# A fused decoder layer: the turns of the MLP's inner rows one cell later, the down projection at the slot's end, its residual in the next slot

## The chip, the cores and the metric

One core of one Trainium2 chip runs the whole kernel. The metric is the device time of one execution in microseconds (us). The engines are PE (TensorE, matmuls; its weight loads are PEld), DVE (VectorE), ACT (ScalarE), POOL (GpSimd) and SP (SyncE, which here only issues transfers). Each runs its own list of instructions in order, and they wait for one another by semaphores. PE writes into eight PSUM banks.

## The reference: what is computed

One decoder layer on x of 8 batches x 512 rows x 512 columns, in float32:

```
x = x + self_attention(layernorm(x))             16 heads of 32, causal, q and k normed per head
x = x + cross_attention(layernorm(x), ctx_1024)  16 heads, softmax over the 32 largest scores
x = x + ffn(layernorm(x))

ffn: gate = silu(bitlinear(x, w_gate)); up = bitlinear(x, w_up)     inner width 2048
     return bitlinear(gate * up, w_down)
bitlinear(x, w): rows of x rounded to 8-bit steps of their largest element, w to -1, 0, 1
```

The inner rows h = gate * up are 2048 wide. The down projection needs each row's largest element over all 2048 before it can round any of them.

## The kernel before

The program is a pipeline written out by hand. Time is cut into **slots** s = -7 to 160. Slot s handles one group of four heads of one tile of 128 query rows in self attention, and of cross attention 20 slots later (`LAG`). A batch is 16 slots. Each slot has eight **cells**, 0 to 7: the even ones carry a head of self attention, the odd ones a head of cross attention. In each cell PE turns the probabilities (`probs`, L595), computes scores (`scores`, L627 to L632), multiplies the head of the cell before by its values (`values`, L609), and then does the **units** that `cells(s)` puts into the cell: projections of q, k and v, turns (transposes) of inputs and of attention results, the output projections, and the MLP's matmuls. Units use two PSUM banks in turn (`shared_ps`), so a unit waits (`freed`) until the unit two before it has been read: mostly by ACT, for the output projections and the down projection by DVE.

The MLP of a row tile t takes three slots (`mlp_step`, r = 0, 1, 2), from slot 37 of a batch's own count on:

- r = 0 and 1: gate and up projections for four chunks of 512 (cells 2 and 6). ACT reads them (L742), POOL completes the silu (`silu`, L1115 and L1117), DVE multiplies by up and finds the maximum (`mlp`, L968 and L971). The last chunk, at cell 6 of r = 1, is finished by POOL and DVE in the following slot, with each row's scale (L977 to L982).
- r = 2, here called the **down slot**: POOL quantises the inner rows in four pieces (`inner_quant`, L1129), PE turns each piece (unit `hT`, L637 with `hh`) in cells 2, 3, 4 and 5, ACT copies them to `hT` (L742), and PE runs the down projection of 16 matmuls in cell 6 (unit `down`, L672). DVE's last step in the slot (`down`, L989) scales it and adds the residual `x2res`. SP stores the result at the start of the next slot (`store_y`, L503).

The down slots are s mod 16 = 7, 10, 13 and 0 for t = 0, 1, 2 and 3. The last batch's MLP runs nearly alone, in slots 149 to 160: the **tail**.

What else stands in these slots matters. On DVE each slot is in the main the search for the 32 largest scores of four heads (`top`, L878 and L883: 32 passes over 128x512). In between come `self_maxima` (L1019), `norms` (L900 and L909, which divide attention results by their sums; they need the values of both kinds of heads up to the last cell of the slot before), `mlp`, `row_scale`, `cross_rows` (L926) and `self_rows` (L939, which adds the input to the output projection of self attention, L656). The self output projection is in cell 3 of slots 14, 15, 0 and 1 mod 16, the turn of its input in cell 2. In slot 0 cell 3 also holds a projection `self_qkv` (L684, 8 matmul records), in slot 10 the cross queries (L703), in slot 7 cells 2 and 3 hold the turns of self keys and queries (L707), and in slot 13 cell 5 holds the cross values (L696). The order of DVE's steps in a slot is this list:

```
top(c, 0, FIRST_MAX)
self_maxima(s - 1, 1)
top(c, 0, ROUND_1)
sum_squares(s)
norms(s)
mlp(s - 1, False)
top(c, 0, ROUND_2)
...
```

SP's list in a slot: inputs, the stores of x1 and x2, `store_y` of the slot before, the residual loads `x1res` and `xres`, the residual load `x2res` of a down slot, the weights, and the copies of turned keys and queries to their stacks (`copy_part`, L513, 32 transfers in a slot that has them).

Of the kernel before, what the change touches and what calls it, by code (L numbers as in the profile page):

```python
# [16 lines left out]
NB, S, D = 8, 512, 512  # L17
# [9 lines left out]
SLOTS = NG * NT  # L27
# [4 lines left out]
RING = 3  # L32
REPLACED = -3e38
LAG = 20
FIRST, LAST = -7, SLOTS * (NB - 1) + LAG + 28
CELLS = 2 * HG
NS = NB * SLOTS
NTILES = NB * NT
# [30 lines left out]
def cross_tile(s):  # L69
    return tile_at(s, LAG + 15)  # L70
# [44 lines left out]
def mlp_down(s):  # L115
    t, r = mlp_step(s)
    return [t] if t is not None and r == 2 else []


def cells(s):  # L120

    u = [[] for _ in range(CELLS)]
    g, q = self_group(s), s % NT
    if g is not None:
        for at, cell, unit in ((0, 0, ("self_qkv", g, 0)), (0, 3, ("self_qkv", g, 1)), (0, 6, ("self_qkv", g, 2)),
                               (1, 1, ("self_qkv", g, 3)), (3, 2, ("self_kT", g)), (3, 3, ("self_qT", g))):
            if at == q:
                u[cell].append(unit)
    g = cross_group(s)
    if g is not None:  # L130
        for at, cell, unit in ((1, 5, ("cross_v", g)), (2, 0, ("cross_kT", g)), (2, 3, ("cross_qT", g))):
            if at == q:
                u[cell].append(unit)
    if cross_tile(s) is not None:
        u[0].append(("cross_oT", cross_tile(s)))
        u[1].append(("cross_out", cross_tile(s)))
    if x1_tile(s) is not None:
        u[1].append(("feed", "x1", x1_tile(s)))
    if self_tile(s) is not None:
        u[2].append(("self_oT", self_tile(s)))  # L140
        u[3].append(("self_out", self_tile(s)))
    if x2_tile(s) is not None:
        u[4].append(("x2T", x2_tile(s)))
    for early, cell in ((True, 2), (False, 6)):
        for t, n in mlp_chunk(s, early):
            u[cell] += [("gate", t, n), ("up", t, n)]
    for t in mlp_down(s):
        for n in range(NF):
            u[2 + n].append(("hT", t, n))
        u[6].append(("down", t))  # L150
    for k, f in enumerate(feeds(s)):
        u[5 + k].append(("feed", *f))
    return u
# [108 lines left out]
def decoder_layer(nc, x, ctx_in, W_attn, b_attn, W_proj, b_proj, q_gamma, q_beta, k_gamma, k_beta,  # L262
# [10 lines left out]
    with ExitStack() as keep:  # L273
# [77 lines left out]
        hT = sb("hT", [P, KF, P], BF16)  # L351
# [14 lines left out]
        def pipeline():  # L366
            C = Counts()
# [51 lines left out]
            for s in slots:  # L419
                t = self_tile(s)  # L420
                if t is not None:
                    for k in ("x1", "stats", "aggr"):
                        C.plan("x1_stats", (k, t))
                    for k in range(5):
                        C.plan("x1_norm", (t, k))
                t = x2_tile(s)
                if t is not None:
                    for k in ("amax", "clip", "inv"):
                        C.plan("dve_rows", (k, t))
                    for k in range(3):  # L430
                        C.plan("pool_rows", ("quant", t, k))
                t = cross_tile(s)
                if t is not None:
                    for k in ("x2", "stats", "aggr"):
                        C.plan("dve_rows", (k, t))
                    for k in range(6):
                        C.plan("pool_rows", ("ln", t, k))
                for early, at in ((False, s - 1), (True, s)):
                    for t, n in mlp_chunk(at, early):
                        C.plan("h_pool", ("t1", t, n))  # L440
                        C.plan("h_pool", ("r", t, n))
                        C.plan("h_dve", ("h", t, n))
                        C.plan("h_dve", ("max", t, n))
                        if n == NF - 1:
                            for k in ("amax", "clip", "inv"):
                                C.plan("h_dve", (k, t))
                            C.plan("h_pool", ("scale", t))
                            for q in range(NF):
                                C.plan("h_pool", ("q", t, q))
                for t in mlp_down(s):  # L450
                    C.plan("h_dve", ("out", t))

            def freed(eng, u):

# [25 lines left out]
            with nc.Block() as block:  # L480
                @block.sync
                def _(sp):
# [18 lines left out]
                    def store_y(t):  # L501
                        sp.wait_ge(h_dve, upto("h_dve", ("out", t)))
                        sp.dma_start(rows(out_rows, t), x2res[:]).then_inc(y_out, step("y_out", t, 16))  # L503
# [15 lines left out]
                    for s in slots:  # L519
                        done += len(feeds(s - 1))  # L520
                        while pending and ring[pending[0]] - RING < done:
                            load_feed(pending.pop(0))
                        t = x1_tile(s)
                        if t is not None:
                            sp.wait_ge(x1_stats, upto("x1_stats", ("x1", t)))
                            sp.dma_start(rows(x1_rows, t), xres[:]).then_inc(x1_out, step("x1_out", t, 16))
                        t = x2_tile(s)
                        if t is not None:
                            sp.wait_ge(dve_rows, upto("dve_rows", ("x2", t)))
                            sp.dma_start(rows(x2_rows, t), x2t[:]).then_inc(x2_out, step("x2_out", t, 16))  # L530
                        for t in mlp_down(s - 1):
                            store_y(t)
                        t = cross_tile(s)
                        if t is not None:
                            if t:
                                sp.wait_ge(dve_rows, upto("dve_rows", ("x2", t - 1)))
                            sp.wait_ge(x1_out, upto("x1_out", t, 16))
                            sp.dma_start(x1res[:], rows(x1_rows, t)).then_inc(x1res_in, step("x1res_in", t, 16))
                        t = self_tile(s)
                        if t is not None:  # L540
                            if t:
                                sp.wait_ge(x1_out, upto("x1_out", t - 1, 16))
                                sp.wait_ge(x1_norm, upto("x1_norm", (t - 1, 4)))
                            sp.dma_start(xres[:], rows(x_rows, t)).then_inc(xres_in, step("xres_in", t, 16))
                        for t in mlp_down(s):
                            sp.wait_ge(x2_out, upto("x2_out", t, 16))
                            if t:
                                sp.wait_ge(y_out, upto("y_out", t - 1, 16))
                            sp.dma_start(x2res[:], rows(x2_rows, t)).then_inc(x2res_in, step("x2res_in", t, 16))
                        for at, which, g, before in loads:  # L550
                            if at == s:
                                load_weights(which, g, before)
                        mine = [u for cell in cells(s) for u in cell if u[0] in STACKED]
                        if mine:
                            k_unit, q_unit = mine
                            for unit, j in ((k_unit, 0), (k_unit, 1), (q_unit, 0), (q_unit, 1),
                                            (k_unit, 2), (q_unit, 2), (k_unit, 3), (q_unit, 3)):
                                copy_part(unit, j)
                    for t in mlp_down(LAST):
                        store_y(t)  # L560
                    sp.wait_ge(x1_out, 16 * NTILES)
                    sp.wait_ge(x2_out, 16 * NTILES)
                    sp.wait_ge(y_out, 16 * NTILES)
# [301 lines left out]
                def _(dve):  # L865
# [156 lines left out]
                    for s in slots:  # L1022
                        c = s - LAG
# [3 lines that stand above are left out]
                        sum_squares(s)  # L1027
                        norms(s)
                        mlp(s - 1, False)
                        top(c, 0, ROUND_2)  # L1030
                        row_scale(s)
                        cross_rows(s)
                        top(c, 0, ROUND_3)
                        top(c, 1, FIRST_MAX)
                        self_maxima(s, 0)
                        self_rows(s)
                        top(c, 1, ROUND_1)
                        feed_stats_of(s + 1)
                        top(c, 1, ROUND_2)
                        mlp(s, True)  # L1040
                        top(c, 1, ROUND_3)
                        down(s)

                @block.gpsimd
                def _(pool):
# [424 lines left out]
```

## Time and profile before

| | |
|---|---|
| median of 3 runs | 4032.62 us (4030.38 to 4032.8) |
| the profiled execution | 4034.79 us, its span 4033.0 us |
| busy: PE, DVE, ACT, POOL | 3329.4, 3343.9, 2450.5, 1796.7 us |
| mean granted TensorE clock | 0.859 of full speed |
| chain that ended last, by engine | DVE 40%, PE 25%, POOL 13%, issue 11% |

The span is cut by the profile into instructions on each engine with start, duration, and what ended the idle time before them. "A <- B" means that A's engine stood idle until B was done. Idle time of an engine costs only where the end of the program hangs on that engine, so each wait has to be looked at in its place. The granted clock is the share of TensorE's full clock of 2.4 GHz that it was given.

### The profile page before, as it was taken

The numbers are of one execution on the slowest core, as the hardware profiler recorded it, in microseconds if no ns is written. First come the engines' busy times: TensorE is split into PE (matmuls) and PEld (weight loads), VectorE is DVE, ScalarE is ACT, GpSimd is POOL, SyncE is SP. The second block draws the span as 40 slices with busy tenths as digits, with TensorE's granted clock in tenths as the row PEclk, the third lists the DMA queues.
The fourth block names the chain that finished last, engine by engine and source line by source line (L and its number), as shares of the span: only waits on it lengthen the run. The fifth ranks groups of instructions, "written<-read, shape, count | busy, mean of one in ns | idle before, by whom it ended". The sixth has DMA issues, their size and how long they took to land.

```text
span 4033.0 us, 61337 instructions
## 1 busy us (share of the span) xinstructions
PE 3329.4 (83%) x18502; PEld 2434.3 (60%) x18502; DVE 3343.9 (83%) x7699; ACT 2450.5 (61%) x4921; POOL 1796.7 (45%) x2316
## 2 busy tenths in 40 slices
PE   2587898998989898998899888997899888877775
PEld 2365576666666666666666666666666666555542
DVE  4312299999999899899989999999989999999962
ACT  3344476666766567666766676666766676455533
POOL 0123244445654555444544555445544554344433
PEclk7768888888988899888988898898988898877767
DMA  7122322322222212222223222222232221211100
GB/s 271 52 54 64 99 64 76 84 77 60 77 77 72 70 49 79 79 73 69 74 77 84 63 71 67 74 65 62 77 89 79 58 66 43 61 45 35 32 21 19
DMA packets 167443, 283.04 MB, mean 70 GB/s; under 512 B 40639, under 2 KB 52939, under 8 KB 166606
## 3 DMA queue, kind: packets, MB, share of 16 engines
q1 hardware_dynamic: 160782, 275.98, 25.1%
q10 hardware_dynamic: 6336, 3.15, 0.3%
q8 instruction: 153, 2.51, 0.3%
q14 instruction: 172, 1.41, 0.1%
HBM read 113.27 MB, written 31.46 MB: 36 GB/s over the span
## 4 chain that ended last, share of the span: by engine, by line
DVE 40%; PE 25%; POOL 13%; issue 11%; ACT 4%; SPq 3%; DMA 1%; DVEq 0%; POOLq 0%; ACTq 0%
DVE cW L883 17%; DVE top L878 13%; PE bank L684 5%; PE bank L656 4%; PE bank L609 4%; POOL srs L1149 4%; SPq L513 3%; PE bank L672 2%; DVE smx L1019 2%; PE bank L637 2%; POOL cS L1170 2%; PE bank L595 2%; DVE hh L968 2%; POOL hh L1117 1%; DVE hmx L971 1%
## 5 line engine op out<-in xcount | busy, mean ns | idle before, releaser
L883 DVE MATCH_REPLACE8 cW<-top,cW 128x512 f32<-128x512 f32 x1536 | 1026.8, 676 | 0.0
L878 DVE MAX8 top<-cW 128x8 f32<-128x512 f32 x1536 | 981.4, 681 | 0.0
L799 ACT ACTIVATE PT<-bank 128x512 f32<-128x512 f32 (+3 forms) x1024 | 537.9, 525 | 356.5 <-PE bank L595 353.1
L1170 POOL TENSOR_TENSOR cS<-cS,cW 128x512 f32<-128x512 f32 x512 | 667.7, 1325 | 185.4 <-ACT cW L827 185.3
L609 PE MATMUL bank<-cv,PT 128*128 128x33 f32 x4096 | 585.0, 290 | 138.7 <-ACT PT L799 138.1
L609 PEld LDWEIGHTS bank<-cv,PT 128*128 128x128 f32 x4096 | 552.8, 209 | 176.5 <-ACT PT L799 170.2
L1177 POOL TENSOR_SCALAR cnb<-top 128x2 f32<-128x2 f32 x256 | 49.0, 191 | 938.1 <-DVE top L878 924.3
L609 PEld LDWEIGHTS bank<-sv,PT 128*128 128x128 f32 x2560 | 397.4, 211 | 82.2 <-ACT PT L799 59.6
L827 ACT ACTIVATE cW<-cW,cnb 128x512 f32<-128x512 f32 x512 | 348.7, 737 | 110.5 <-DVE cW L883 110.3
L684 PE MATMUL bank<-w_group,xT 128*128 128x384 f32 x1024 | 411.6, 550 | 0.0
L609 PE MATMUL bank<-sv,PT 128*128 128x33 f32 x2560 | 373.3, 280 | 36.7 <-ACT PT L799 35.6
L595 PE MATMUL bank<-ident,cS 128*128 128x128 f32 x2048 | 350.1, 298 | 63.2 <-POOL cS L1170 63.2
L821 ACT ACTIVATE cS<-cS,cnb 128x512 f32<-128x512 f32 x512 | 379.6, 741 | 16.1 <-DVE cW L883 16.1
L1019 DVE TENSOR_REDUCE smx<-sP 128x2 f32<-128x256 f32 (+3 forms) x256 | 205.9, 804 | 212.7 <-ACT sP L808 212.7
L1163 POOL TENSOR_TENSOR part<-part 128x512 fp32r<-128x512 f32 x128 | 168.3, 1315 | 451.1 <-ACT part L742 450.9
L595 PEld LDWEIGHTS bank<-ident,cS 128*128 128x128 f32 x2048 | 279.9, 162 | 116.7 <-POOL cS L1170 67.3
L883 DVE MATCH_REPLACE8 cW<-top,cS 128x512 f32<-128x512 f32 x512 | 342.5, 677 | 0.0
L878 DVE MAX8 top<-cS 128x8 f32<-128x512 f32 x512 | 327.2, 681 | 5.7 <-ACT cS L808 5.7
L814 ACT ACTIVATE sP<-sP,snb 128x384 f32<-128x384 f32 (+3 forms) x512 | 294.9, 578 | 35.5 <-POOL snb L1184 34.8
L808 ACT ACTIVATE cS<-bank 128x512 f32<-128x512 f32 x512 | 311.8, 609 | 1.6 <-PE bank L632 1.6
L684 PEld LDWEIGHTS bank<-w_group,xT 128*128 128x128 f32 x1024 | 205.2, 211 | 137.2 <-issue 40.3
L632 PE MATMUL bank<-ck_stack,cq_stack 128*128 128x512 f32 x512 | 269.1, 526 | 5.8 <-ACT cS L808 4.4
(151 smaller groups left out, 6092.4 us busy)
## 6 DMA issues: line engine op xcount, KB each, us to landing
sk_stack<-part SPq DMA_DIRECT2D x512, 64.0 KB, 2.0
sq_stack<-part SPq DMA_DIRECT2D x512, 64.0 KB, 2.0
ck_stack<-part SPq DMA_DIRECT2D x512, 64.0 KB, 2.0
cq_stack<-part SPq DMA_DIRECT2D x512, 64.0 KB, 2.0
w_group<-wa_by_group SPq DMA_DIRECT2D x32, 768.0 KB, 4.5
w_group<-wc_by_group SPq DMA_DIRECT2D x32, 768.0 KB, 4.3
feed<-in_x SPq DMA_DIRECT2D x32, 256.0 KB, 2.9
feed<-in_ctx SPq DMA_DIRECT2D x32, 256.0 KB, 3.0
```

The costliest lines, as they stand in the source:

```text
L595: mm = pe.transpose(turned_ps[C.parity("turned_full", label)][:, k * P:(k + 1) * P], p[:, k * P:(k + 1) * P], ident[:])
L609: mm = pe.matmul(o[:, j * (HD + 1):(j + 1) * (HD + 1)], pt[:, k * P:(k + 1) * P], v[m // NT % len(v)][:, k, j, :], start=k == 0, stop=k == ...
L684: mm = pe.matmul(ps[:, 0:3 * P], xT[:, c, t * P:(t + 1) * P], w_group[:, c, :], start=False, stop=c == NC - 1, skip_group_check=True)
L799: act.activation(PT[k][:, 0:n], turned_ps[k][:, 0:n], ACT.Copy).then_inc(turned_read, step("turned_read", label))
L808: act.activation(dst, score_ps[k][:, 0:n], ACT.Copy).then_inc(score_read, step("score_read", label))
L814: act.activation(p, p, ACT.Exp, bias=snb[:, j:j + 1], scale=SCALE).then_inc(sexp, step("sexp", (m, j)))
L821: act.activation(cS[c % 2][j][:], cS[c % 2][j][:], ACT.Exp, bias=cnb[c % 2][:, j:j + 1], scale=SCALE).then_inc(cexp, step("cexp", (c, j)))
L827: act.activation(cW[j][:], cW[j][:], ACT.Exp, bias=cnb[c % 2][:, j:j + 1], scale=SCALE).then_inc(crest, step("crest", (c, j)))
L878: dve.max(top8[:, j, r, :], src[:]).then_inc(topk, step("topk", (c, r, "max", j)))
L883: dve.match_replace(cW[j][:], top8[:, j, r, :], src[:], REPLACED).then_inc(topk, step("topk", (c, r, "replace", j)))
L1019: dve.reduce_max(smx[:, 2 * half:2 * half + 2], sP[half][:, :, 0:n], AXX).then_inc(smax, step("smax", (s, half)))
L1170: pool.tensor_tensor(cS[m % 2][j][:], cS[m % 2][j][:], cW[j][:], ALU.subtract).then_inc(cprob, step("cprob", (m, j)))
```

## The change

The units `hT` of a down slot move from cells 2 to 5 to cells 3 to 6, and the unit `down` from cell 6 to cell 7, the last. DVE's out step for it moves from the end of the down slot to the next slot, behind `norms` and `mlp(s - 1, False)`. SP's store moves with it, to the end of that next slot. The pipeline gets one slot more (to 161) for the last out step.

```
-FIRST, LAST = -7, SLOTS * (NB - 1) + LAG + 28
+FIRST, LAST = -7, SLOTS * (NB - 1) + LAG + 29
...
     for t in mlp_down(s):
         for n in range(NF):
-            u[2 + n].append(("hT", t, n))
-        u[6].append(("down", t))
+            u[3 + n].append(("hT", t, n))
+        u[7].append(("down", t))
...
+                for t in mlp_down(s - 1):
+                    C.plan("h_dve", ("out", t))
                 for early, at in ((False, s - 1), (True, s)):
...
-                for t in mlp_down(s):
-                    C.plan("h_dve", ("out", t))
...
                             sp.dma_start(rows(x2_rows, t), x2t[:]).then_inc(x2_out, step("x2_out", t, 16))
-                        for t in mlp_down(s - 1):
-                            store_y(t)
                         t = cross_tile(s)
...
                                 copy_part(unit, j)
-                    for t in mlp_down(LAST):
-                        store_y(t)
+                        for t in mlp_down(s - 1):
+                            store_y(t)
...
                         mlp(s - 1, False)
+                        down(s - 1)
                         top(c, 0, ROUND_2)
...
                         top(c, 1, ROUND_3)
-                        down(s)
```

The instructions are the same ones in another order; line numbers fall by two. On **PE, slot 80** (third batch, t = 3), from the turn of the self output (`so`) in cell 2 on; `hh` is a turn of inner rows, `cS` and `sP` are probabilities. Before:

```order
L637 MATMUL bank<-ident,so 128x128 x4
L637 MATMUL bank<-ident,hh 128x128 x4
L595 MATMUL bank<-ident,cS_1 128x128 x4
L632 MATMUL bank<-ck_stack,cq_stack 128x512
L609 MATMUL bank<-sv,PT 128x33 x4
L681 MATMUL bank<-bias,ones 128x128 x3
L684 MATMUL bank<-w_group,xT 128x384 x4
L653 MATMUL bank<-bias,ones 128x512
L656 MATMUL bank<-wproj,oT 128x512 x4
L637 MATMUL bank<-ident,hh 128x128 x4
```

After:

```order
L635 MATMUL bank<-ident,so 128x128 x4
L593 MATMUL bank<-ident,cS_1 128x128 x4
L630 MATMUL bank<-ck_stack,cq_stack 128x512
L607 MATMUL bank<-sv,PT 128x33 x4
L679 MATMUL bank<-bias,ones 128x128 x3
L682 MATMUL bank<-w_group,xT 128x384 x4
L651 MATMUL bank<-bias,ones 128x512
L654 MATMUL bank<-wproj,oT 128x512 x4
L635 MATMUL bank<-ident,hh 128x128 x4
```

The first turn of `hh`, which stood in front of cell 3, now stands behind its projection (L684, now L682) and the self output projection (L656, now L654).

On **PE at the end of slot 80**, before:

```order
L681 MATMUL bank<-bias,ones 128x128 x3
L684 MATMUL bank<-w_group,xT 128x384 x4
L672 MATMUL bank<-wdT,hT 128x512 x16
L637 MATMUL bank<-ident,feed 128x128 x4
L595 MATMUL bank<-ident,cS_3 128x128 x4
L632 MATMUL bank<-ck_stack,cq_stack 128x512
L609 MATMUL bank<-sv,PT 128x33 x4
```

After:

```order
L682 MATMUL bank<-w_group,xT 128x384 x4
L635 MATMUL bank<-ident,hh 128x128 x4
L635 MATMUL bank<-ident,feed 128x128 x4
L593 MATMUL bank<-ident,cS_3 128x128 x4
L630 MATMUL bank<-ck_stack,cq_stack 128x512
L607 MATMUL bank<-sv,PT 128x33 x4
L670 MATMUL bank<-wdT,hT 128x512 x16
```

The 16 matmuls on `wdT` leave cell 6; the last turn of `hh` takes their place, and they stand behind the last cell's scores and values, in front of the next slot's probabilities.

On **DVE, from the end of slot 80 into slot 81**, before:

```order
L883 MATCH_REPLACE cW<-top,cW 128x512 x2
L989 SCALAR_TENSOR_TENSOR x2res<-bank,hcol,x2res 128x512
L878 MAX top<-cS_0 128x8
L878 MAX top<-cS_1 128x8
L1019 TENSOR_REDUCE smx<-sP 128x2
L883 MATCH_REPLACE cW<-top,cS_0 128x512
L883 MATCH_REPLACE cW<-top,cS_1 128x512
L878 MAX top<-cW 128x8 x2
L900 RECIPROCAL rr<-bank 128x8
L909 TENSOR_TENSOR so<-bank,rr 128x128
L909 TENSOR_TENSOR co<-bank,rr 128x128
L883 MATCH_REPLACE cW<-top,cW 128x512 x2
```

After:

```order
L881 MATCH_REPLACE cW<-top,cW 128x512 x2
L876 MAX top<-cS_0 128x8
L876 MAX top<-cS_1 128x8
L1017 TENSOR_REDUCE smx<-sP 128x2
L881 MATCH_REPLACE cW<-top,cS_0 128x512
L881 MATCH_REPLACE cW<-top,cS_1 128x512
L876 MAX top<-cW 128x8 x2
L898 RECIPROCAL rr<-bank 128x8
L907 TENSOR_TENSOR so<-bank,rr 128x128
L907 TENSOR_TENSOR co<-bank,rr 128x128
L987 SCALAR_TENSOR_TENSOR x2res<-bank,hcol,x2res 128x512
L881 MATCH_REPLACE cW<-top,cW 128x512 x2
```

The out step (`x2res`) stands behind norms (L909, now L907), nine rows later.

On SP, in slot 78 for example, the store of `out_y` (L503) stands behind the load of `xres` (L544, now L542) and the 32 copies of keys and queries (L513), where it stood in front of them.

## Rows read from the trace of the kernel before

**Rows 1.** The page, part 1: busy us, share of the span, instructions.
```profile
PE 3329.4 (83%) x18502; PEld 2434.3 (60%) x18502; DVE 3343.9 (83%) x7699; ACT 2450.5 (61%) x4921; POOL 1796.7 (45%) x2316
```

**Rows 2.** Waits, whole span: engine line waited for, us in total, times, longest.
```profile
PE bank L637 <- POOL hh L1129: 165.1, 32, 9.3
...
DVE xres L939 <- PE bank L656: 103.2, 29, 7.0
...
DVE x2res L989 <- PE bank L672: 78.9, 27, 11.0
```

**Rows 3.** Line 989, window 840 to 3830: durations min/median/max, first, last; then its waits.
```profile
L989 DVE SCALAR_TENSOR_TENSOR x2res<-bank,hcol,x2res x28: 745/751/752, 985.1 to 3825.3; 128x512 f32<-128x512 f32 x28
...
  PE bank L672: 35.3, 23
```

**Rows 4.** Timeline of PE, slot 80: start, us, line, tiles, [idle before <-releaser].
```profile
2097.53 0.63 PE L637 MATMUL bank<-ident,hh 128*128 128x128 f32 x4 [2.24 <-POOL hh L1129]
...
2100.25 5.49 PE L684 MATMUL bank<-w_group,xT 128*128 128x384 f32 x8
...
2106.16 3.70 PE L656 MATMUL bank<-wproj,oT 128*128 128x512 f32 x8
...
2116.23 2.85 PE L684 MATMUL bank<-w_group,xT 128*128 128x384 f32 x8
```

**Rows 5.** Timeline of DVE, slots 48, 112, 128 and the end of 80.
```profile
1222.45 0.69 DVE L939 TENSOR_TENSOR xres<-bank,xres 128x512 f32<-128x512 f32 x1 [5.61 <-PE bank L656]
...
2122.57 0.75 DVE L989 SCALAR_TENSOR_TENSOR x2res<-bank,hcol,x2res 128x512 f32<-128x512 f32 x1 [2.21 <-PE bank L672]
...
2127.27 0.19 DVE L900 RECIPROCAL rr<-bank 128x8 f32<-128x8 f32 x1
...
2997.28 0.69 DVE L939 TENSOR_TENSOR xres<-bank,xres 128x512 f32<-128x512 f32 x1 [5.60 <-PE bank L656]
...
3432.05 0.69 DVE L939 TENSOR_TENSOR xres<-bank,xres 128x512 f32<-128x512 f32 x1 [3.73 <-PE bank L656]
```

**Rows 6.** Windows in slot 80: length, busy by engine, PEclk, DMA share, GB/s.
```profile
2095.30:2099.20 3.90, 1.67 (x15) 1.66 (x15) 3.80 (x12) 2.15 (x6) 3.65 (x6) 1.00 0.11 16
2099.20:2106.10 6.90, 6.90 (x16) 3.41 (x15) 5.09 (x12) 1.50 (x5) 0.58 (x3) 0.51 0.19 73
```

**Rows 7.** Timeline of PE, slot 87.
```profile
2300.14 1.09 PE L637 MATMUL bank<-ident,hh 128*128 128x128 f32 x4 [8.66 <-POOL hh L1129]
```

**Rows 8.** Timeline, PE and DVE, slots 90 and 91.
```profile
2376.63 1.09 PE L637 MATMUL bank<-ident,hh 128*128 128x128 f32 x4 [3.62 <-POOL hh L1129]
...
2394.09 0.75 DVE L989 SCALAR_TENSOR_TENSOR x2res<-bank,hcol,x2res 128x512 f32<-128x512 f32 x1 [1.33 <-PE bank L672]
...
2398.17 0.09 DVE L883 MATCH_VALUE_LOAD cW<-top,cS 128x8 f32 x1 [0.48 <-POOL cS L1170]
...
2400.47 0.28 DVE L909 TENSOR_TENSOR co<-bank,rr 128x128 f32<-128x128 f32 x1
...
2401.23 0.64 PE L707 MATMUL bank<-ident,sx 128*128 128x128 f32 x4
```

**Rows 9.** Timeline, PE and DVE, slots 77 and 78.
```profile
2010.25 1.09 PE L637 MATMUL bank<-ident,hh 128*128 128x128 f32 x4 [5.14 <-POOL hh L1129]
2012.70 1.09 PE L637 MATMUL bank<-ident,hh 128*128 128x128 f32 x4
...
2026.44 0.75 DVE L989 SCALAR_TENSOR_TENSOR x2res<-bank,hcol,x2res 128x512 f32<-128x512 f32 x1 [0.32 <-PE bank L672]
...
2032.95 0.28 DVE L909 TENSOR_TENSOR co<-bank,rr 128x128 f32<-128x128 f32 x1
...
2034.88 0.63 PE L637 MATMUL bank<-ident,so 128*128 128x128 f32 x4
...
2046.56 0.69 DVE L939 TENSOR_TENSOR xres<-bank,xres 128x512 f32<-128x512 f32 x1 [4.95 <-PE bank L656]
```

**Rows 10.** Line 989, window 3930 to 4033: its waits.
```profile
  PE bank L672: 43.6, 4
```

## The prediction

> **What bounds the kernel now.** I read the page first: PE and DVE are both busy 83% of the span [rows 1], so neither alone explains the time, and an edit that only moves work pays only where one of the two waits for the other. The list of waits is next [rows 2]. Three of its rows belong to the piece of program that moves: PE waits 165.1 us for POOL's quantised inner rows before it turns them, DVE waits 103.2 us for the output projection of self attention, and 78.9 us for the down projection. Which of these lies on the path is seen slot by slot in the timeline. The slots repeat by the batch: the same wait comes at 1222.45 and, four batches on, at 2997.28 [rows 5], a period of 443.7 us for 16 slots. A batch has four down slots, s mod 16 = 7, 10, 13 and 0, for the row tiles t = 0 to 3. 28 of the 32 down steps lie in the full slots, and there DVE waits 35.3 us for them [rows 3]; the other four are the last batch's, in the tail: 43.6 us [rows 10].
>
> In each of these down slots PE comes to the first turn at cell 2 while POOL has not quantised yet, and stands: 2.24 us in slot 80 [rows 4], 8.66 in 87 [rows 7], 3.62 in 90 [rows 8], 5.14 in 77 [rows 9]. Everything of PE behind it is late: in slot 80 the self output projection ends at 2106.16 + 3.70 = 2109.86, and DVE stands 5.6 us for it (five such slots, 5.61 to 5.58, and a sixth with 3.73), then 2.21 us for the down projection [rows 5]. These are DVE's only gaps in that slot, so in slot 80 DVE follows PE.
>
> **The change, part by part.** No instruction is added or removed; what is priced is order.
>
> *The turns move one cell back.* At cell 2 PE goes on to cell 3 instead of standing. What it gains is the work of cell 3 that now fits in front of POOL's answer, at most the stall. In slot 80 cell 3 holds two projections, 5.49 and 3.70 us [rows 4], more than the stall, so all 2.24 us go. In slot 90 it holds the projection of the cross queries, 8 matmuls of 512, so the 3.62 us go too. In slot 77 it is small: between the first and the second turn lie 2012.70 - 2010.25 = 2.45 us, 1.09 of them the turn itself [rows 9], so 1.4 us are gained and 3.7 us of stall stay. In slot 87 some 3 of the 8.66 us go; DVE does not follow PE there.
>
> *The clock in slot 80.* From 2095.3 to 2099.2, the stretch with the stall, PE is busy 1.67 of 3.90 us; in the 6.9 us after it the granted clock is 0.51, the lower level of 1.2 GHz [rows 6], and a projection of 8 matmuls takes 5.49 us where the same one takes 2.85 later [rows 4]. With the stall gone PE is busy through that stretch. Bounds for what this gives: 0 (the clock falls all the same) and 5.49 - 2.85 = 2.64 us. I take 2.64, because no other stall stands in front of the fall in this slot.
>
> *Slots 0 and 1, where DVE follows PE, gain what PE gains*: 2.24 + 2.64 = 4.9 us. DVE could take 5.61 + 2.21 = 7.8; the rest comes back as a wait at the reciprocal of norms in the next slot (at 2127.27 in [rows 5]), which needs attention values that PE computes after the down projection. Five such slots give 24.4 us. The sixth waited 3.73 us, the bound; I take 3. Together **27.4 us**.
>
> *The residual moves to the next slot.* Where DVE waits at its end only for the down projection, and PE has caught up by the next slot's norms, the wait goes in full; the 0.75 us instruction only changes slot. Of the 35.3 us, five waits of 2.21 (11.1) are those of slots 0, counted above, and six of 0.3 to 0.5, like the 0.32 in [rows 9] (2.5 in all), are slots 13. The other 35.3 - 11.1 - 2.5 = **21.7 us** are slots 7 and 10 (1.33 in [rows 8]). DVE has next to no gap in slots 8 to 13, so it keeps them.
>
> *Slots 13 and 14.* DVE follows PE again, to the 4.95 us wait in slot 78 [rows 9]: the gain is PE's 1.4 us, the 0.32 included. But the 3.7 us of stall that stay can draw a fall of the clock onto the value projection of cell 5. Bounds: 1.4 - 2.64 = -1.2 us (a loss as in slot 80) and 4.95 (the whole wait goes). I take half of 1.4, 0.7 us, nearest to the turn's own rows, six times: **4.2 us**. By the Trainium skill's page TensorE: Matmul & The Clock Gate, Part 1, the throttled state is the default and activity releases it; by that rule the remaining stall costs clock, each of these slots is at its lower bound, and the sum is 11 us smaller.
>
> *POOL.* In slot 90 PE turns and projects the next inputs earlier, POOL's chain behind them comes earlier, and DVE's 0.48 us wait for POOL's subtraction in slot 91 goes [rows 8], six times: **2.9 us**.
>
> *What could come onto the path: the bank.* The down projection's PSUM bank is now free only after DVE's out step, which comes behind norms, and PE's second unit after the down projection needs it. In slot 78 norms end at 2032.95 + 0.28 = 2033.2; DVE is 0.32 + 0.75 us earlier there, and with the 0.75 of the out step it is done at about 2033.0. PE reaches the unit, the turn of the self output, at 2034.88 [rows 9], or 1.4 us earlier: 0.5 us of cover. In slot 91 norms end at 2400.75, less 1.33 + 0.75, plus 0.75: 2399.4, and PE's turn of the keys is at 2401.23 [rows 8]: 1.8 us, against a lead that grows by up to 3.6. So PE is never later there than today, only its new lead can be cut: cost 0. The Trainium skill's page PSUM — Partial Sum Buffer, section Summary: rules for kernel authors, says "Evacuate promptly"; that speaks against holding a bank for some 6 us, and is the last rival below.
>
> *SP and the ends.* On SP the store of the result moves behind the residual load of self attention and behind the 32 part copies of slots 11 and 14. The next user of its buffer is a load two slots later, and the loads it stood in front of are freed: 0. In the tail the MLP's steps follow each other as before, so the four waits [rows 10] stay: 0. The added slot 161 holds only the last out step and store, which ended the program before too: 0.
>
> **Sum.** 27.4 + 21.7 + 4.2 + 2.9 = 56.2 us. The profiled execution took 4034.8 us, which gives 3978.6; it lies 2.2 us over the median of the runs, so the median comes to **3976 us**.
>
> **Rivals.**
> - *The clock falls all the same* (0.2). For: no row shows that this stall, and not the slot's load, lowered it. Then 5 x 2.24 + 2 = 13.2 instead of 27.4, and 0 instead of 4.2: 3976 + 18.4 = 3995 us.
> - *More than PE's own gain* (0.12): PE, earlier from slot 77 on, takes the rest of the 4.95 us wait in slots 14 as well, 6 x 4.25 = 25 us more: 3951 us. For: that wait is as long as the stall in slot 77 [rows 9]. Against: nothing in PE's work gets shorter.
> - *The waits return elsewhere* (0.1): DVE, early at norms in slots 8 and 11, stands there for the values behind the down projection. Then only what PE gains is left, 13.2 + 4.2 = 17.4: 4015 us. Against: PE is 3 us ahead there.
> - *It does nothing* (0.05): each wait that goes reappears before the slot ends: 4032 us.
> - *Slower* (0.06), by the held bank: PE stands at its second unit until DVE's out step. It decides once PE is the bound behind that point and its lead (3.6 us) exceeds the cover (0.5 to 1.8, about 1.2): 2.4 us in each of 28 down slots are 67 us against 56 gained, 4043 us. Against: only in slots 0 and 13 does DVE follow PE, and PE's lead is smaller there.
>
> **Numbers.** The forecast has the remaining 0.47. To hold 8 in 10, the range reaches over the first rival with slots 13 at their lower bound, and to the second: **3948 to 4010**. About 0.2% (8 us) can be told from no change in this kernel. Faster by over that: 0.47 + 0.2 + 0.12 + 0.1 = 0.89; within it 0.05; slower 0.06.
>
> **What would show it.** Right: PE's wait for POOL before the inner turns falls from 165 us to about 100, with none left in slots 0 and 10; the wait for the self output projection in slots 0 goes from 5.6 us to under 1, with the clock at 1.0; DVE's wait for the down projection is gone outside the tail; a wait of 1 to 3 us at the reciprocal appears in slots 1; the period falls from 443.7 to about 437 us. Wrong: a PE wait of over 1 us for DVE's out step in the slots after down slots, or the projection in slot 0 still at 5.5 us.

## The result, and the profile after

The changed kernel takes 3981.3 us (median of 4 runs, 3970.9 to 3984.7); the kernel before takes 4031.5 us (median of 4). The ratio is 0.9872, 95% interval 0.9852 to 0.9892: 50 us or 1.3% faster. The forecast was 3976 us, range 3948 to 4010. The profiled execution of the changed kernel is its fastest run, 3970.9 us (span 3968.7), 64 us below that of the kernel before, so slot times read from the two traces add up to more than the 50 us of the medians.

The waits of the whole span, with the columns of [rows 2]:

```profile
PE bank L635 <- POOL hh L1127: 97.4, 19, 9.3
...
DVE xres L937 <- PE bank L654: 81.1, 21, 8.0
...
DVE x2res L987 <- PE bank L670: 43.2, 4, 11.7
```

Line numbers are two lower than before. PE's wait for the quantised rows falls from 165.1 to 97.4 us, and 13 of its 32 occasions are gone. DVE's wait for the down projection is down from 78.9 to the 43.2 us of the tail. The wait for the self output projection falls by only 22.1 us in all, but in slots 0 it is gone: there it was 31.7 us in six slots before, five of about 5.6 and one of 3.73. In slots 14 it grew by 10.4 us, in slots 1 by 3.3. Where the out step stands now, line 987 over 840 to 3830 us ([rows 3] before):

```profile
L987 DVE SCALAR_TENSOR_TENSOR x2res<-bank,hcol,x2res x28: 741/741/750, 988.4 to 3765.7; 128x512 f32<-128x512 f32 x28
its engine sat idle before it (us, times) until:
who waited for it (us, times):
  PEld bank L705: 4.6, 5
  PE bank L705: 3.9, 5
...
  PE bank L662: 2.7, 2
...
  PE bank L635: 1.3, 1
```

Nothing is waited for in front of it any more, and PE now waits for it: 3.9 us in five slots 11, and 4.0 us in three slots near the end (123, 129 and 139). The prediction had named a PE wait of over 1 us there as a sign of being wrong; three of the eight are (1.03, 1.88 and 1.25 us).

Slot 80 as PE's timeline shows it, from the turn of the self output on ([rows 4]):

```profile
2072.15 0.63 PE L635 MATMUL bank<-ident,so 128*128 128x128 f32 x4
...
2074.47 2.85 PE L682 MATMUL bank<-w_group,xT 128*128 128x384 f32 x8
...
2077.57 3.70 PE L654 MATMUL bank<-wproj,oT 128*128 128x512 f32 x8
...
2081.10 0.60 PE L635 MATMUL bank<-ident,hh 128*128 128x128 f32 x4
```

There is no stall, and the first projection takes 2.85 us, not 5.49. The windows of slots 77 and 80 say what the clock was (columns as in [rows 6]; the granted clock is the third number from the end). Before:

```profile
2002.17:2027.10 24.93, 19.79 (x129) 16.17 (x128) 24.44 (x60) 12.78 (x30) 12.78 (x16) 0.86 0.10 33
...
2088.65:2123.24 34.59, 32.35 (x174) 22.23 (x173) 26.53 (x63) 16.77 (x38) 12.82 (x20) 0.90 0.20 58
```

After:

```profile
1978.59:2002.46 23.87, 19.26 (x117) 16.79 (x116) 23.70 (x60) 13.64 (x32) 12.78 (x16) 0.79 0.14 45
2066.14:2092.07 25.93, 25.72 (x158) 19.31 (x158) 25.69 (x62) 16.69 (x38) 12.83 (x20) 1.00 0.28 77
```

Slot 80 runs at the full 2.4 GHz; slot 77 runs longer at 1.2 GHz than before. The lower clock now reaches the value projection behind the first turn of inner rows. Before, the first of its four pieces took as long as the others:

```profile
2016.44 1.16 PE L696 MATMUL bank<-w_group,ctxT 128*128 128x128 f32 x8
```

After, the first turn, the first two pieces, and DVE's wait in slot 78, which was 4.95 us before ([rows 9]):

```profile
1986.68 1.08 PE L635 MATMUL bank<-ident,hh 128*128 128x128 f32 x4 [4.30 <-POOL hh L1127]
...
1992.58 1.99 PE L694 MATMUL bank<-w_group,ctxT 128*128 128x128 f32 x8
...
1994.65 1.16 PE L694 MATMUL bank<-w_group,ctxT 128*128 128x128 f32 x8
```

```profile
2024.42 0.69 DVE L937 TENSOR_TENSOR xres<-bank,xres 128x512 f32<-128x512 f32 x1 [6.79 <-PE bank L654]
```

In the table a slot is the time from its first `top` pass on DVE to the next slot's, in the batch of slots 68 to 83. Slots 0 and 1 are 80 and 81 there, in the profile of each kernel.

| slots mod 16 | before | after | difference | forecast |
|---|---|---|---|---|
| 0 and 1 | 34.6 + 23.6 | 25.9 + 27.0 | -5.2 | -4.9 |
| 7 and 8 | 35.9 + 24.3 (34.7 + 24.3 in most batches) | 30.7 + 24.1 | -5.3 (-4.2 in most) | -1.9 |
| 10 and 11 | 26.5 + 25.7 (27.7 + 25.7 in some) | 25.6 + 25.7 | -0.8 or -2.1 | -0.5 to -1.8 |
| 13 and 14 | 24.9 + 31.2 | 23.9 + 33.7 | +1.5 | -0.7 |
| period, mean of four | 443.7 | 433.6 | -10.1 | about -9 |

### The profile page after: what moved, and what is told of

It is laid out like the page before. It is cut to its first block, busy times and chain, and to the rows that moved or that the text cites. A ratio compares the mean times of both kernels' runs of the same rounds, so it can differ in the third digit from the quotient of the medians.

```text
span 3968.7 us, 61337 instructions
## 1 busy us (share of the span) xinstructions
PE 3343.2 (84%) x18502; PEld 2462.5 (62%) x18502; DVE 3333.4 (84%) x7699; ACT 2460.3 (62%) x4921; POOL 1789.4 (45%) x2316
## 4 chain that ended last, share of the span: by engine, by line
DVE 42%; PE 26%; issue 10%; POOL 10%; ACT 4%; SPq 3%; DMA 1%; DVEq 0%; POOLq 0%; ACTq 0%
DVE cW L881 18%; DVE top L876 14%; PE bank L682 6%; PE bank L607 5%; PE bank L654 4%; SPq L513 3%; POOL srs L1147 3%; PE bank L593 2%; DVE smx L1017 2%; PE bank L670 2%; DVE hh L966 2%; PE bank L635 2%; POOL cS L1168 1%; DVE hmx L969 1%; POOL hh L1115 1%
## 5 line engine op out<-in xcount | busy, mean ns | idle before, releaser
L607 PE MATMUL bank<-cv,PT 128*128 128x33 f32 x4096 | 600.0, 294 | 126.0 <-ACT PT L797 125.3
L607 PEld LDWEIGHTS bank<-cv,PT 128*128 128x128 f32 x4096 | 569.9, 214 | 161.9 <-ACT PT L797 155.4
L682 PE MATMUL bank<-w_group,xT 128*128 128x384 f32 x1024 | 406.3, 545 | 0.0
L593 PEld LDWEIGHTS bank<-ident,cS 128*128 128x128 f32 x2048 | 283.9, 164 | 124.0 <-POOL cS L1168 78.9
L812 ACT ACTIVATE sP<-sP,snb 128x384 f32<-128x384 f32 (+3 forms) x512 | 294.1, 577 | 36.0 <-POOL snb L1182 35.3
L682 PEld LDWEIGHTS bank<-w_group,xT 128*128 128x128 f32 x1024 | 202.8, 209 | 134.6 <-issue 35.4
```

Source lines behind the costliest of these rows:

```text
L593: mm = pe.transpose(turned_ps[C.parity("turned_full", label)][:, k * P:(k + 1) * P], p[:, k * P:(k + 1) * P], ident[:])
L607: mm = pe.matmul(o[:, j * (HD + 1):(j + 1) * (HD + 1)], pt[:, k * P:(k + 1) * P], v[m // NT % len(v)][:, k, j, :], start=k == 0, stop=k == ...
L682: mm = pe.matmul(ps[:, 0:3 * P], xT[:, c, t * P:(t + 1) * P], w_group[:, c, :], start=False, stop=c == NC - 1, skip_group_check=True)
L812: act.activation(p, p, ACT.Exp, bias=snb[:, j:j + 1], scale=SCALE).then_inc(sexp, step("sexp", (m, j)))
```

## The experiments

Each run was timed against the kernel before on the same chip; the ratios are to that, so they compare across chips. The changed kernel itself is 0.9872.

### The parts apart: e1 and e2

e1 puts the four turns back; the down projection stays in cell 7 and its residual in the next slot.

```
-            u[3 + n].append(("hT", t, n))
+            u[2 + n].append(("hT", t, n))
```

> The changed kernel with the four turns put back to cells 2 to 5; the down projection stays in cell 7 and its residual in the next slot. My theory (the turns' place gives slots 0 and 1 their 5 us a batch by PE's stall and clock, the residual's place gives slots 7 and 10 theirs): the xres wait of 5.6 us and the lower clock in slots 0 return, the loss in slots 13 and 14 (1.4 us a batch against before) goes, so 3981 + 27 - 8 = about 4000 us. Rival 1 (the residual's place gives all of it): 3981 us, and slots 0 without the xres wait. Rival 2 (the turns give all of it): 4030 us.

Measured: 4013.6 us beside 4037.6, ratio 0.9948 (0.9935 to 0.9961). e2 is the opposite, the kernel before with only the cells changed:

```
-            u[2 + n].append(("hT", t, n))
-        u[6].append(("down", t))
+            u[3 + n].append(("hT", t, n))
+        u[7].append(("down", t))
```

> The kernel before with turns in cells 3 to 6 and the down projection in cell 7; its residual stays at the end of the same slot, where DVE now waits for the last thing that PE does in the slot. My theory: slots 0 keep the 2.2 us of stall and 2.6 us of clock but give 1.9 us back at the slot's end, slots 7 and 10 keep about 1.5 and 1.3 us, slots 13 get worse: about 3995 us. Rival (only the removed wait matters): 4030 us or slower.

Measured: 4011.9 us, ratio 0.9942 (0.9929 to 0.9956). So neither part alone gives the result: 0.5% and 0.6%, 1.3% together. The two add up to 1.1%, and the difference to 1.3% is not clear of the intervals. My 4000 and 3995 us were both too good: they stand for gains of 31 and 36 us, 68 together, where the whole change gives 50. In e1 the stall in slot 80 is back, with a granted clock of 0.89 in the slot:

```profile
2084.23:2115.86 31.63, 29.38 (x160) 21.27 (x161) 25.78 (x62) 17.15 (x39) 12.83 (x20) 0.89 0.22 63
```

The xres wait there is 5.61 us again; and the late PE also makes POOL late, so DVE waits some 2.3 us for POOL's subtraction in slots 11, 0.5 us before (27.9 us instead of 25.7 in slot 91). In e2 DVE waits for what now is PE's last work in the slot. Line 989 in e2 over 840 to 3830 us, against 35.3 us before ([rows 3]):

```profile
  PE bank L672: 58.0, 20
```

So each part pays alone, and each makes one wait longer that the other takes away again.

### Slots 0 alone: e3, and the clock alone: e11

e3 is e1 with the turns of row tile 3 one cell later.

```
+            u[2 + (t % NT == 3) + n].append(("hT", t, n))
```

> As e1, but the turns of row tile 3 (slots 0) are one cell later, as in the changed kernel; those of tiles 0 to 2 in cells 2 to 5. It tells what slots 0 and 1 alone are worth: my theory 27 us below e1, so about 3973 to 3976 us, with the clock at 1.0 in slots 0. Rival (the clock falls in slots 0 by the load, not by the stall): 13 us below e1.

Measured: 3988.5 us, ratio 0.9885 (0.9873 to 0.9898), 25.1 us below e1 where 27 were expected and 13 by the rival. Slots 0 and 1 take 52.9 us in place of e1's 58.1. With 0.9885 e3 also lies inside the changed kernel's interval: in sum, the turns' move gives little outside slots 0. e11 leaves everything of the kernel before where it was and gives PE something to do in that stall:

```
                         elif kind == "hT":
+                            if u[2] == 0 and u[1] % NT == 3:
+                                for _ in range(16):
+                                    pe.transpose(ps[:, 0:P], ident[:], ident[:])
                             pe.wait_ge(h_pool, upto("h_pool", ("q", u[1], u[2])))
```

> The kernel before, with 16 extra turns of the identity (1.7 us) in the 2.24 us stall at the first turn of inner rows in slots 0, nothing moved. It parts the two terms of slots 0. Theory: the stall stays, the clock stays at 1.0, the xres wait in slots 0 falls from 5.6 to about 3 us: 13 us less than before, 0.9967. Rival (the clock falls in slots 0 by the slot's load): as before, 1.000.

Measured: 4012.6 us beside 4036.1, ratio 0.9939 (0.9927 to 0.9952): 23.5 us where 13 were expected, for a kernel that only does more. The window of slot 80, and DVE's wait in it:

```profile
2085.62:2116.95 31.33, 30.91 (x189) 22.60 (x189) 26.55 (x64) 16.76 (x38) 12.85 (x20) 1.00 0.23 64
```

```profile
2103.60 0.69 DVE L942 TENSOR_TENSOR xres<-bank,xres 128x512 f32<-128x512 f32 x1 [2.32 <-PE bank L656]
```

The clock is 1.00 and the wait 2.32 instead of 5.61: of slot 0's loss 3.3 us a batch were the clock, and the empty stall at the first turn brought it down, since nothing else was changed. The 2.3 us that are left are as long as the stall itself (2.24).

### Why slots 13 and 14 lost: e4, e8, e9, e5

e4 is the changed kernel with the turns of row tile 2 back in cell 2.

```
-            u[3 + n].append(("hT", t, n))
+            u[2 + (t % NT != 2) + n].append(("hT", t, n))
```

> The changed kernel with the turns of row tile 2 alone (slots 13) back in cells 2 to 5. In the changed kernel the wait for the self output projection in slots 14 grew from 4.95 to 6.8 us. Theory clock (the stall that stays in slot 13 draws 10 us of half clock over work that stood behind it before): that wait falls back, 8 us less in all, about 3973 us. Rival bank (PE is held in slot 14 by DVE's out step or by the down projection in cell 7): nothing changes, 3981 us.

Measured: 3978.1 us beside 4037.6, ratio 0.9852 (0.9839 to 0.9865), which overlaps with the changed kernel's 0.9872. The wait in slot 78 is 6.77 us, as in the changed kernel (6.79) and not as in the kernel before (4.95). As a test it was poorly chosen, since PE stands in cell 2 again, for 2.47 us in slot 77 and 5.12 us in slot 61. But two of its slots say more than its time. In slots 77 and 109 the stall is the same 2.47 us, and the turn that ends it still runs at the full clock (0.63 us). Behind it the clock falls in slot 77 (0.86 over the slot, all of the lower stage over work), and DVE waits 6.77 us in slot 78; in slot 109 it stays at 1.00, and DVE waits 3.54 us in slot 110. So slots 14 hang on the clock, and not on the turn's cell.

Where the lower clock falls counts as much as how long it lasts. The kernel before has 0.86 in slot 77 too, but its clock was low already in the stall: 0.69 over the 5.14 us of standing and 0.71 over the 6.2 us of work behind it, which is 3.2 us of lower clock in the stall and 3.6 over work. The changed kernel has 0.70 over the 4.30 us of its stall, 0.50 over the next 5.9 us and 0.57 over 2.1 more: 2.6 us in the stall and 7.7 over work. The same projection took 5.49 us at 1.2 GHz and 2.85 at 2.4 GHz, so 4.1 us more of such work cost about 2.0 us; less the 0.84 us by which the stall shrank, that is an estimate of 1.2 us lost, where 1.5 were measured.

e3 had shown it too. In its trace the same slots 13 and 14 come with two clocks, in different batches: windows of slots 77 and 109, and the xres waits in slots 78 and 110:

```profile
1984.93:2008.79 23.86, 19.79 (x114) 17.45 (x114) 23.69 (x60) 12.38 (x29) 12.81 (x16) 0.79 0.13 45
2857.99:2881.85 23.86, 20.65 (x136) 16.91 (x135) 23.69 (x60) 15.26 (x35) 12.78 (x16) 0.93 0.13 45
```

```profile
2031.82 0.69 DVE L937 TENSOR_TENSOR xres<-bank,xres 128x512 f32<-128x512 f32 x1 [7.87 <-PE bank L654]
...
2902.08 0.69 DVE L937 TENSOR_TENSOR xres<-bank,xres 128x512 f32<-128x512 f32 x1 [5.00 <-PE bank L654]
```

One program, one order: 0.79 goes with 7.87 us, 0.93 with 5.00 (the stall itself differs here, 4.07 and 3.21 us). e8 tests it by filling the stall in slots 13 of the changed kernel, with the same kind of lines as in e11, in front of the same wait:

```
+                            if u[2] == 0:
+                                for _ in range({2: 32}.get(u[1] % NT, 0)):
+                                    pe.transpose(ps[:, 0:P], ident[:], ident[:])
```

> The changed kernel; in slots 13 PE does 32 extra turns of the identity (about 3.5 us) into the bank that the first turn of inner rows then overwrites, just where it stands 4.3 us for POOL. They change no result. Theory (PE's stall lowers the clock, and that is what slots 13 and 14 lost): no lower clock in slots 13, the wait for the self output projection in slots 14 falls from 6.8 to about 3.6 us, about 19 us less in all: 0.9825 of the time before. Rival (the clock falls by something else, or the loss is the down projection in cell 7): as the changed kernel, 0.987, or slower by the extra work.

Measured: 3955.9 us beside 4035.0, ratio 0.9804 (0.9789 to 0.9819), 27 us less than the changed kernel's share of that chip's time (3983), where 19 were expected; the two profiled executions are 21 us apart, and all of it is in slots 14. Slot 77 in the window, and DVE's wait in slot 78:

```profile
1972.07:1995.94 23.87, 23.57 (x175) 19.74 (x175) 23.70 (x60) 15.87 (x37) 12.82 (x16) 1.00 0.14 46
```

```profile
2016.03 0.69 DVE L940 TENSOR_TENSOR xres<-bank,xres 128x512 f32<-128x512 f32 x1 [4.92 <-PE bank L654]
```

Slot 14 is 31.8 us here and 30.0 to 30.8 in the other five batches, against 33.2 to 33.8. With slot 13 that is 0.4 us less than before here and up to 2.2 in the others. So the loss was the clock, drawn by the stall that stayed.

e9 fills the stall of slots 7 too: `{0: 44, 2: 32}` in the same line.

> As the run before, and 44 such extra turns in slots 7 as well, where PE stands over 5 us. Theory: the 24 us of lower clock in slots 7 become shorter, but DVE does not follow PE there, so the time stays within 3 us of the run before. Rival (PE's clock in slot 7 sets the pace of POOL and DVE behind it): 5 us or more less.

Measured: 3957.0 us, ratio 0.9804 (0.9791 to 0.9817): nothing more, as expected. The mean granted clock rose from 0.868 to 0.874, in a place where DVE does not follow PE. A higher clock is worth nothing by itself.

e5 fills the stall of slots 13 with the kernel's own work, the value projection two cells earlier:

```
-            for at, cell, unit in ((1, 5, ("cross_v", g)), ...
+            for at, cell, unit in ((1, 3 if s % SLOTS == 13 else 5, ("cross_v", g)), ...
```

> The changed kernel with the cross value projection of slots 13 in cell 3 instead of 5, in front of the first turn of inner rows: the kernel's own work fills the stall. Theory: its weights arrive some 2.6 us after PE is there, so part of the stall stays; PE gains 1.6 us and perhaps the clock: between 8 and 20 us less than the changed kernel, 0.983 to 0.985. Rival (the weights are late and the turns wait longer than before): 0.99.

Measured: 3972.1 us beside 4035.0, ratio 0.9841 (0.9827 to 0.9854), 12 us less than the changed kernel by the ratios, inside the band; the two intervals just touch. But slots 14 still take 30.1 to 35.4 us from batch to batch, and PE still falls to the lower clock in slots 13 (0.80 to 0.93). The kernel's own work fills the stall only in part: in slot 77 PE stands 2.28 us for the projection's weights instead. Which share of the 12 us is clock and which is order stays open.

### The price of the held bank: e7 and e12

e7 moves the out step behind the first half of the search:

```
-                        down(s - 1)
                         top(c, 0, ROUND_2)
                         row_scale(s)
                         cross_rows(s)
                         top(c, 0, ROUND_3)
+                        down(s - 1)
```

e12, below, puts it behind one round of the search only:

```
-                        down(s - 1)
                         top(c, 0, ROUND_2)
+                        down(s - 1)
```

> The changed kernel with DVE's out step behind the whole first half of its slot's search instead of behind norms, 5.5 to 8 us later. It prices the held bank. In the changed kernel PE waits 0.8 us for the out step in slots 11 and has 2.3, 3.5 and 4.3 us to spare in slots 1, 14 and 8. Theory: 5.5 to 8 us later PE stands 2 to 7 us in each of the four slots, and slots 1 and 14, where DVE follows PE, pass 3 to 6 us each on: 35 to 70 us slower than the changed kernel, 0.996 to 1.004. Rival (PE catches up everywhere before DVE needs it): 0.987.

Measured: 4107.6 us beside 4035.0, ratio 1.0179 (1.0165 to 1.0193): slower than the kernel before, by 3.1% of it (124 us) slower than the changed one, and nearly twice the most that I had expected. Who waits for the out step in e7, 840 to 3830 us:

```profile
  PE bank L705: 42.3, 5
  PE bank L635: 42.1, 12
  PE bank L662: 30.6, 9
```

115 us in 26 slots. Slots 1 grew from 27.0 to 34.4 us, 9 from 27.8 to 32.7, 11 from 25.7 to 30.8 and 14 from 33.7 to 37.6. I had counted only slots 1 and 14 as passing it on; but 8 and 11 pass it on too. PE, held 2.0 us in slots 8, leaves DVE standing 3.7 us at the reciprocal in slot 73 (0.6 in the changed kernel); held 8.7 us in slots 11, it is late for POOL's silu, for which DVE waits 4.2 us in slot 75 (nothing in the changed kernel).

> The changed kernel with DVE's out step one round of the search later (2.7 us). In e7, 6 to 8 us later, PE waited 118 us for it and the time rose by about 124 us against the changed kernel. Theory (PE's spare time of 2.3, 3.5 and 4.3 us in slots 1, 14 and 8 covers 2.7 us but for 0.4 us; slot 11 waits 3.5 us): 5 to 15 us slower than the changed kernel, 0.989 to 0.991. Rival (the cost is in proportion, 2.7 of 6.8 us): 50 us slower, 0.9995.

Measured: 3992.2 us beside 4036.1, ratio 0.9887 (0.9873 to 0.9900): 6 us above the changed kernel, and not the 50 of proportion. In the same view PE waits for it:

```profile
  PE bank L705: 21.5, 5
...
  PE bank L662: 8.9, 3
...
  PE bank L635: 4.1, 3
```

34.5 us of waiting on PE cost about 6, known to some 10 us either way, which still leaves out the rival's 50. With 2.7 us more PE stands in slots 11 (up to 4.9 us) and hardly elsewhere before slot 123, and a batch's slots 11 and 1 grow by 0.8 and 0.4 us. At 6 to 8 us it stands behind 26 of the 28 out steps.

### A version that beats both: e10

e10 is e8 with a second filling, in front of PE's wait for POOL's subtraction in slots 3 and 7:

```
+                            if j == 0 and s % SLOTS in (3, 7):
+                                free("turned_read", turned_read, label)
+                                for _ in range(30):
+                                    pe.transpose(turned_ps[...][:, 0:P], ident[:], ident[:])
                             pe.wait_ge(cprob, upto("cprob", (m, j)))
```

> e8 (the changed kernel with its stall in slots 13 filled) and 30 extra turns of the identity, 3.3 us, where PE stands 3.7 to 4.6 us in slots 3 and 7 for POOL's subtraction behind its long power. They change no result. Theory: the lower clock in slots 2 and 3 goes, the 2.1 us wait for the cross output projection in slots 3 with it; slots 7 give nothing, as in e9: 10 to 15 us less than e8, 0.977. Rival (there the wait is POOL's and the clock no matter): as e8, 0.9804, or slower by what the turns overrun the stall.

Measured: 3937.3 us beside 4036.1, ratio 0.9753 (0.9739 to 0.9766), 2.5% faster than the kernel before. By the ratios that is 20 us less than e8, by the profiled executions 13, where 10 to 15 were expected. But the gain came in another place: the lower clock in slots 3 went only in part (0.69 in e8, here 0.72 in slot 83 and 0.86 in slot 99), and DVE's wait in front of the step that reads the cross output projection did not go (in slot 83 2.07 us in e8, 2.47 here). What fell is the wait for the residual load one slot later: all slots 4 together are 15 us shorter, and slots 14 are 5 us longer. In slot 84 the wait is 4.14 us in e8 and here

```profile
2166.95 0.69 DVE L931 TENSOR_TENSOR x2t<-bank,x1res 128x512 f32<-128x512 f32 x1 [0.37 <-DMA x1res<-x_rows]
```

That load stands on SP behind the part copies of the slot before, and those wait for PE, ACT and POOL. That the clock brings them forward is my reading; no run here parts it.

## Why the prediction was right, and where it was not

**Slots 0 and 1** were right in mechanism and nearly in size, 4.9 us forecast and 5.2 measured. The clock term was sized too small: 2.64 us from one projection, 3.3 by e11, because the rest of PE's work in that stretch is slowed as well (0.6 us in slot 80's timeline). Of DVE's 7.8 us some came back in the next slot, at the reciprocal, where it was forecast, and also at the self output projection there, which had been waited for 0.32 us before:

```profile
2097.98 0.21 DVE L898 RECIPROCAL rr<-bank 128x8 f32<-128x8 f32 x1 [1.79 <-issue]
...
2108.66 0.69 DVE L937 TENSOR_TENSOR xres<-bank,xres 128x512 f32<-128x512 f32 x1 [1.17 <-PE bank L654]
```

**Slots 7 and 10** were right in kind: the wait for the down projection went in full, 1.9 us of the 4.2 in slots 7 and 8. Two gains there were not in the sum. DVE's first wait for POOL's subtraction in slot 7 was 2.32 us and is 0.94. It comes and goes with the batch in most of the kernels, also where the turns stand as before (e3); its cause was not tested. And DVE's multiplication by up in slots 8 (L968, now L966) takes 0.68 us and not 1.50: before, it ran at the same time as a subtraction on POOL (2333.63 and 2333.31 us in slot 88), and in the changed kernel the two do not overlap (2302.70 and 2304.32). e1 has the 0.68 too, so this came with the residual's move; the prediction did not have it. For slots 10 and 11 e1 shows that they needed the turns' move as well: without it the two take 53.5 us and not 51.3. Without the turns' move DVE's waits for POOL in slots 11 rise to 2.3 us, which the prediction had not seen.

**Slots 13 and 14** are the step that failed. I took 0.7 us gained, "half of 1.4", between bounds of -1.2 and 4.95; measured is a loss of 1.5 us, just beyond the lower bound. The clause in front of the number named the cause ("the 3.7 us of stall that stay can draw a fall of the clock onto the value projection of cell 5"), and e8 confirms it. By the Trainium skill's page TensorE: Matmul & The Clock Gate, Part 1, the throttled state is the default and activity releases it; the trace agrees here, with a granted clock of 0.79 in slot 77 behind the stall that stayed. The stall also shrank by 0.84 us (5.14 to 4.30), not by 1.4: the 1.4 was read from work at the lower clock.

**POOL's 0.48 us** in slots 11 went, and as time. Slot 11 is as long as before (25.7 us) although it now holds the out step's 0.75 us, which slot 10 lost; the pair is 0.8 us shorter where DVE had not waited for the down projection.

**The bank** cost nothing that the trace shows, as forecast: PE's lead is cut in slot 11 by 0.8 us and in no other full slot of this batch, and DVE waits for nothing in that slot. That three such waits are over 1 us was listed as a sign of being wrong; the time came out as forecast all the same. The rival had its mechanism right and its threshold about right (2.7 us later is nearly free, 6 to 8 us costs 124 us), so it was a real danger and its chance of 0.06 rested on the cover alone.

**The sum** of 56.2 us came out at 50 by the medians and 64 by the profiled executions. In these, over the slots from 36 to 146, slots 0 and 1 gave 31 us (27.4 forecast), 7 and 8 gave 28 (15.8 of the 21.7), 10 and 11 gave 11 (8.8 with POOL's), and 13 and 14 lost 8 (4.2 gained by forecast). So two errors cancel, 12 us too much in slots 13 and 14 and 12 too little in slots 7 and 8, and that the sum came so close is in part luck. One number in the list of signs did not follow from the sum: the period was to fall to "about 437 us", while the terms give about 9 us a batch, 435; it fell to 433.6.

## What to carry to other kernels

When two engines are equally busy, price a move by which of them the other follows in each stage: a stall less or a faster clock on PE reached the time in slots 0 and 13 (e11, e8), and a faster clock in slots 7 gave nothing (e9). Do not price each half of a change by the whole of a wait that both shorten: my two halves were forecast at 31 and 36 us and gave about 21 and 23. Behind a stall of TensorE look at the granted clock before counting the stall alone; filling it with work whose result is overwritten is a cheap test of that, and here it was also a gain of 0.7%. Before a PSUM reader is moved later, measure the slack of the next user of its bank: inside it the move was free, little beyond it (e12) the cost stayed small, and far beyond it (e7) 115 us of waiting cost 124.

## What the runs showed that I had not expected

A kernel that only does more can be faster: 16 added turns in a stall, eight times a run, took 0.6% off the kernel before, and 32 and 30 in three kinds of stall took the changed one from 0.987 to 0.975. And equal batches of one execution differ by 2.8 us in one slot (34.7 and 31.9 us in e3) by how much of the preceding slot was at the lower clock, so a difference of 1 or 2 us in one slot of one batch says little.
